# Two transformer layers on one core: a new out-projection, third norm, hand-over and routed block

## What is computed

```python
# layer 0
xn = layernorm(x)
x  = x + attn0(xn) + ffn0(xn)   # 32 query heads, 8 key heads of 64, window 64, rms norm, rotation; gated quantised ffn of 704
# layer 1
xn = layernorm(x)
Xn = layernorm(xn) * ln_w + ln_b
x  = x + (softmax(rope(Q) rope(K)^T / 4) V) W_out + xn \
       + routed(xn)             # attn1: 16 heads of 16, all 1024 keys
# routed: w = xn W_r + b_r; of each batch the 64 rows with the largest w;
#   rows with w above the 64th value become w * (gelu(x W1 + b1) W2 + b2), all others stay x
```

## Time and profile before

| what | value |
|---|---|
| median of 3 runs | 1092.83 us (1084.54, 1092.83, 1093.44) |
| the profiled execution | 1086.89 us, its span 1085.1 us |
| busy | PE 943.4, DVE 862.2, POOL 698.1, ACT 687.0 us |
| mean granted TensorE clock | 0.958 |

### The profile page before, as it was taken

The page is one execution under the profiler, slowest core; times in us unless marked ns, Lnnn a source line. Parts: engine busy times, 40 slices in busy tenths (PEclk is TensorE's granted clock), DMA queues, the critical chain, the costliest instruction groups (busy, mean ns, idle before and its releaser), DMA issues. The chain is left out here.

```text
span 1085.1 us, 26423 instructions
## 1 busy us (share of the span) xinstructions
PE 943.4 (87%) x8729; PEld 529.8 (49%) x8729; DVE 862.2 (79%) x1777; ACT 687.0 (63%) x1786; POOL 698.1 (64%) x1001
## 2 busy tenths in 40 slices
PE   3588997998988988989889887379999999999998
PEld 2355665665766656656667654243222222333233
DVE  6797888888887887887888883358999999888952
ACT  2555655655565655655656552016999999888974
POOL 4677888888888887887887882422655565332220
PEclk9698999999999999999999998579999999999999
DMA  5646544544444434444534432521121211311001
GB/s 193 126 106 123 108 90 86 97 83 91 95 82 90 96 81 91 97 79 88 102 80 87 93 82 52 166 65 21 22 42 21 40 22 22 50 31 36 7 2 39
DMA packets 241611, 81.00 MB, mean 75 GB/s; under 512 B 215812, under 2 KB 240068, under 8 KB 241220
## 3 DMA queue, kind: packets, MB, share of 16 engines
q1 hardware_dynamic: 238980, 74.85, 33.7%
q10 hardware_dynamic: 2496, 4.46, 1.2%
HBM read 18.49 MB, written 4.19 MB: 21 GB/s over the span
## 5 line engine op out<-in xcount | busy, mean ns | idle before, releaser
L1259 DVE TENSOR_REDUCE l_mxv<-l_mx 128x1 f32<-128x1024 f32 x256 | 294.9, 1217 | 28.1 <-PE l_mx L1462 28.1
L1170 ACT ACTIVATE l_prob<-l_sc 128x512 f32<-128x512 f32 x512 | 272.9, 604 | 30.1 <-PE l_sc L1470 29.1
L389 ACT ACTIVATE an<-an 128x256 f16<-128x256 f32 x128 | 53.3, 416 | 210.9 <-DVE an L563 210.5
L708 POOL TENSOR_TENSOR t<-t 128x320 f32<-128x320 f32 x128 | 110.3, 862 | 106.7 <-DVE t L610 106.5
L1462 PE MATMUL l_mx<-l_kt,l_qt 48*128 48x512 f16 x512 | 155.4, 386 | 13.6 <-DVE l_mxv L1259 13.6
L1470 PE MATMUL l_sc<-l_qt,l_kt 50*128 50x512 f16 x512 | 156.8, 384 | 0.4 <-ACT l_prob L1170 0.4
L699 POOL TENSOR_TENSOR rm<-ss,half_neg 128x5 f32<-128x5 f32 x128 | 155.9, 1218 | 0.0
L1441 PE MATMUL l_acc<-l_prob,qkv_all 128*17 128x256 f32 x2048 | 154.5, 386 | 0.0
L867 PE MATMUL ob<-wo_hi,ats 128*128 128x256 f16 x512 | 109.0, 280 | 32.8 <-DMA ats<-an 27.3
L1332 POOL TENSOR_SCALAR l_mxs<-l_mxv 128x8 f32<-128x8 f32 x32 | 7.5, 235 | 179.4 <-DVE l_mxv L1259 179.4
L812 PE MATMUL pv<-v,probs 128*64 128x65 f32 x2048 | 89.2, 230 | 30.0 <-ACT probs L438 23.0
(11 more groups left out here) (180 smaller groups left out, 2147.3 us busy)
## 6 DMA issues: line engine op xcount, KB each, us to landing
qkv_all<-w_qkv SPq DMA_DIRECT2D x3, 768.0 KB, 8.6
v<-v SPq DMA_DIRECT2D x64, 32.5 KB, 1.9
xn_all<-xs SPq DMA_DIRECT2D x16, 128.5 KB, 2.2
xa<-x SPq DMA_DIRECT2D x16, 128.0 KB, 2.4
tk<-nat SPq DMA_TRANSPOSE x128, 2.7
qkv_all<-w_o SPq DMA_DIRECT2D x8, 256.0 KB, 3.8
ats<-an SPq DMA_TRANSPOSE x128, 2.3
xc<-x SPq DMA_DIRECT2D x16, 128.0 KB, 2.5
```

Of the source, the lines that this page charges most:

```text
L389: return act.activation(dst, src, ACT.Copy, scale=scale)
L708: pool.tensor_tensor(t1[:, b, :, :], t1[:, b, :, :], t2[:, :, :], ALU.add).then_inc(s_["pool_u"], 1)
L1170: act.activation(prob[:, (y * NI + u) % NPR, h * 512:(h + 1) * 512], sc[:, k % NSC, :], ACT.Exp, scale=D1 ** -0.5).then_inc(s_["act_sc"], 1)
L1259: dve.tensor_reduce(mxv[:, x % 2, u:u + 1], mx[:, MX[k] % 2, :], AX.X, ALU.max).then_inc(s_["dve_mx"], 1)
```

## The change

1. Third norm: `norm_stats` on `xs` goes. Its variance is worked out from the second inverse root (1 + eps - eps x rs2^2: two DVE instructions on 128x1). `xl1` is one DVE instruction with `rs3` and `ln_w`; POOL keeps the addition of `ln_b`, and DVE has it for the last tile. POOL's rotation of tile 14 is moved by three slots, behind the last `rs3`.
2. Hand-over: the fp16 halves of items' pair 0 (`c = 0, 1`) are made by POOL inside layer 0 and turned by the last two DMAs of its SP queue; their memory is that of layer 0's projection weights (`early`). The small constants are loaded in layer 0 at slot 24. The router column is stored ahead of `xs`.
3. Routed block: thresholds, selection and positions go into slots 5 (`LEVEL_AT`, `PICK_AT`, `THR_AT`, `COUNT_AT`) behind the first maxima. Running sums replace the 28 counting matmuls by 1. The weighted one-hot matrix goes; the block is multiplied by the weight instead and split to fp16. Score banks are used beside `acc`, gelu's table is loaded at the start, `x1s` is loaded in four parts in slots 6 to 9.
4. Projections: POOL writes normalised items 0 to 23 as high and low fp16 halves (`ctx0`, `ctx1`) and splits `W_out`; SP turns them by DMA. Y is at `u == 3` of slots 25 to 32, Z at the eight places of `AHEAD_AT`. C and T go, with the copies behind them.

```diff
-SLOT_O = 25
-SLOT_H = 37
+SLOT_Y = 25
+AHEAD_AT = ((33, 3), (34, 3), (35, 3), (36, 3), (37, 2), (37, 5), (38, 1), (38, 4))
-SPREAD_AT = ((4, 6), (5, 0))
-GATHER_AT = ((5, 1), (5, 2), (5, 3), (5, 4))
-TURN_AT = (5, 6)
-HIDDEN_AT = ((6, 0), (6, 2))
+LEVEL_AT, PICK_AT = (5, 0), (5, 1)
+THR_AT, COUNT_AT = (5, 1), (5, 2)
+GATHER_AT = ((5, 3), (5, 4), (5, 5), (5, 6))
+TURN_AT = (5, 7)
+HIDDEN_AT = ((6, 0), (6, 1), (6, 2), (6, 3))
+SPREAD_AT = ((6, 4), (6, 6))
 RESULT_AT = ((6, 5), (6, 7))
+BLOCK_AT, PARTS_AT = (7, 0), ((7, 2), (7, 4))
...
+                    dve.scalar_tensor_tensor(mv3[:, par, :], rs2[:, par, :], -LN_EPS, rs2[:, par, :], ALU.mult, ALU.mult
+                                             ).then_inc(s_["dve_b3"], 1)
...
+                    dve.tensor_scalar(ve3[:, par, :], mv3[:, par, :], 1.0 + LN_EPS, None, ALU.add).then_inc(s_["dve_v3"], 1)
-                    norm_stats(st3, mv3, ve3, xs[:, par, 0:D], par, "dve_b3", "dve_g3", "dve_v3", n)
...
-                    pool.tensor_tensor(xl1[:, :], xl1[:, :], lnw[:, :], ALU.mult).then_inc(s_["pool_lw"], 1)
...
+                if s == way(NT - 1):
+                    pool.wait_ge(front["set_nq"], 2)
+                    pool.wait_ge(s_["pool_rope"], NT - 1)
+                    for c in range(2):
+                        split(pool, c, qkv1_all, nq, front)
...
+            sp.wait_ge(front["pool_split"], 2)
+            for a, dst in enumerate((qt, kt)):
+                sp.dma_start_transpose(dst[:, 0, :].rearrange("p (i t) -> p i t", i=NI),
+                                       nq[:, 0, a, :, :, :].rearrange("p i h e -> p (i h e)")).then_inc(wq_ld[a * 2], 16)
...
+                if (c, u) == COUNT_AT:
+                    pe.wait_ge(s_["mod_dve"], MOD["run8"])
+                    pe.matmul(counts, bef[:, :], sel, start=True, stop=False)
+                    pe.matmul(counts, ones[:, :], cum, start=False, stop=True).then_inc(s_["mod_pe"], 1)
...
+                pool.tensor_copy(parts[:, :, 0, d:d + D1], ctn[:, b, :, :]).then_inc(s_["pool_part"], 1)
+                pool.wait_ge(s_["pool_part"], t * 2 + 2)
+                pool.tensor_tensor(parts[:, :, 1, d:d + D1], ctn[:, b, :, :], parts[:, :, 0, d:d + D1], ALU.subtract
+                                   ).then_inc(s_["pool_ctx"], 1)
...
                         for j in range(KC):
-                            pe.matmul(mx[:, MX[k] % 2, 0:D], ctt[:, i % 2, j, :], wou[:, j, :], start=(j == 0), stop=False)
-                        pe.matmul(mx[:, MX[k] % 2, 0:D], spread[0:CAP, i, :], blk[0:CAP, :], start=False, stop=True
-                                  ).then_inc(s_["pe_mx"], 1)
+                            for n, (l, w) in enumerate(((0, wou_hi), (0, wou_lo), (1, wou_hi))):
+                                pe.matmul(mx[:, MX[k] % 2, 0:D], ctt0[:, i, l, j, :], w[:, j, :], start=(j == 0 and n == 0), stop=False)
+                        routed(mx[:, MX[k] % 2, 0:D], 0, i).then_inc(s_["pe_mx"], 1)
```

More of the change, by code:

```diff
@@ L90, in build @@
         qkv1_all = ctx.enter_context(nc.sbuf_tensor("qkv1_all", [P, ITEMS * NI * (2 * D1 + VW)], F32))
-        loads = layer0(nc, ctx, idf, idh, ranked, xn2_all, qkv1_all, x, w_qkv, w_o, q_w, k_w, w_gate, w_up, s_gate, s_up, w_down, s_down,
-               ln_w, ln_b, w_in, w_r, b_r, pos_table, masks, eye, out)
-        layer1(nc, loads, idf, idh, ranked, xn2_all, qkv1_all, w_out1, b_r, w1, b1, w2, b2, before, slots, out)
+        early = ctx.enter_context(nc.sbuf_tensor("early", [P, 2 * KC * G * CW], F16))
@@ new lines, in build, with turning @@
+        loads, spare = layer0(nc, ctx, idf, idh, ranked, xn2_all, qkv1_all, early, small, sources, front, x, w_qkv, w_o, q_w, k_w,
+                       w_gate, w_up, s_gate, s_up, w_down, s_down, ln_w, ln_b, w_in, w_r, b_r, pos_table, masks, eye, out)
+        layer1(nc, loads, spare, idf, idh, ranked, xn2_all, qkv1_all, early, small, front, w_out1, w1, w2, out)
+def turning(early):
+    nq = early[:, 0:4 * NI * P].rearrange("p (a j i h e) -> p a j i h e", a=2, j=2, i=NI, h=2)
+    qt = early[:, 4 * NI * P:4 * NI * P + 4 * S].rearrange("p (n s) -> p n s", n=4)
+    kt = early[:, 4 * NI * P + 4 * S:4 * NI * P + 8 * S].rearrange("p (n s) -> p n s", n=4)
+    return nq, qt, kt
@@ L952, in ahead @@
 def ahead(c, u):
-    return (c - SLOT_H) * NI + u
+    return AHEAD_AT.index((c, u)) if (c, u) in AHEAD_AT else None
 def fold_at(c, u):
@@ L985, in max_units, with layer1 @@
                 order.append(("X", c - LAG_X, u))
-            if u == 3 and 0 <= c - SLOT_O - 1 < NI:
-                order.append(("Y", c - SLOT_O - 1))
-            order += [(kind, i) for kind, i in (("Z", ahead(c, u) - 1), ("T", ahead(c, u))) if 0 <= i < NI]
+            if u == 3 and 0 <= c - SLOT_Y < NI:
+                order.append(("Y", c - SLOT_Y))
+            if ahead(c, u) is not None:
+                order.append(("Z", ahead(c, u)))
     return {unit: k for k, unit in enumerate(order)}
-def layer1(nc, loads, idf, idh, ranked, xn2_all, qkv1_all, w_out1, b_r, w1, b1, w2, b2, before, slots, out):
+def layer1(nc, loads, spare, idf, idh, ranked, xn2_all, qkv1_all, early, small, front, w_out1, w1, w2, out):
     SC = score_units()
@@ L1443, in piece, with routed @@
                 ins.then_inc(s_["pe_pv"], 1)
+            def routed(dst, b, i):
+                rows = slice(b * CAP, (b + 1) * CAP)
+                pe.matmul(dst, spread[rows, i, :], blk_hi[rows, :], start=False, stop=False)
+                return pe.matmul(dst, spread[rows, i, :], blk_lo[rows, :], start=False, stop=True)
             for c in range(SLOTS):
```

379 lines of the change are left out of this document (205 added, 174 removed).

## The result

The changed kernel takes **1047.9 us** (median of four: 1043.5, 1047.9, 1047.9, 1049.2) against 1093.1 for the kernel before, timed beside it; the ratio is 0.959 (95% interval 0.954 to 0.963). The prediction was 1048, range 1032 to 1064. Medians here are over all executions of a kernel; ratios and their intervals leave out the slow ones, more than 1.5% above its fastest.

The account below looks back on a forecast made before the run. No engine alone bounded layer 0, a chain of waits the hole behind it, PE the slots with projections; -5.0 (layer 0), -22.6 (head) and -13.7 (projections) make -41.3, from a mean of 1089.4 to 1048 us, range 1032 to 1064.

Parts of the forecast that it names:

- Layer 0's body: Third norm in layer 0's sixteen tiles: shorter DVE work saves 5.0 us in all, bounds 0 and 8.
- so not all arrives: I take 5.5: Third norm, layer 0: of 7.2 us saved on DVE over 16 tiles, 5.5 arrives, as PE is 91% busy.
- POOL's product with `ln_w` I count at nothing: Layer 0's tiles: taking this product, 0.72 us a tile, off POOL gains nothing, since POOL afterwards waits for DVE.
- layer 0 gains nothing: Rival on layer 0's body: PE is its bound, or `xl1` stretches by the shared interface; 1053 us, chance 0.16.
- the rival's price: `xl1` in layer 0: 0.94 us instead of 0.59 by the shared interface, 5.6 us over 16 tiles; that rival's chance 0.16.
- The end of layer 0: Last tile: `rs3` no longer waits for tile 14's rotation, PE transposes at 677.6 instead of 681.79; 4.2 us earlier.
- To the first maxima: Last rotation to first maxima: keys turned inside layer 0, constants' loads and 28 matmuls gone from the wait; -20.7 us.
- Slots 5 to 7: Start of layer 1: +1.1 us to slot 7 with the selection now inside, +1.2 in slot 7 from added DVE instructions.
- half clock through slot 5: Part of the slow-head rival: PE at half clock in slot 5, +6 us; with late transposes 1057 us, chance 0.15.
- Y and Z: Layer 1's projections as fp16 matmuls: Y slots 10.6 us, Z slots 10.3, slot 37 10.8; -13.7 in all.
- five fp16 matmuls, 0.55 + 0.24 = 0.8: Z in slots 33 to 36: each lengthens the 9.52 us slot by 0.8, to 10.3; +3.1 over the four.
- The floor of 9.95: Y slots: the least length, DVE's steady 9.52 us plus one add of 0.42; rival of slots there 1042 us, chance 0.16.

Follow-up runs that it names:

- mult_back: The changed kernel with the third norm's product with `ln_w`, and the last tile's addition of `ln_b`, back on POOL; 1054.8 us, ratio 0.970 to the kernel before.
- y_u6: The changed kernel with Y, and Z of slots 33 to 36, at the slot's seventh place instead of its fourth; 1051.6 us, ratio 0.965 to the kernel before.
- stats_back: The changed kernel with the third norm's statistics computed from the normed row again; 1061.5 us, ratio 0.973 to the kernel before.

## Why the prediction was right, and where not

**Layer 0's body** was mis-sized: -5.0 with bounds 0 and 8, where the marks give -9.0 and the ten middle tiles 0.59 a tile between the two kernels, 8.9 over fifteen. Two steps failed. The first and larger is "so not all arrives: I take 5.5". The statistics alone are worth 0.52 a tile, 7.8 over fifteen: all of the 0.45 a tile that the prediction had found arrives, and a little more. The second is "POOL's product with `ln_w` I count at nothing: it stands in a slot where POOL afterwards waits for DVE". POOL does wait there, 1.16 us in one tile of the changed kernel:

```profile
311.39 0.72 POOL L808 TENSOR_TENSOR xl<-xl,lnb 128x256 f32<-128x256 f32 x1
313.28 0.87 POOL L752 TENSOR_TENSOR t<-t 128x320 f32<-128x320 f32 x1 [1.16 <-DVE t L648]
```

But the wait is for DVE, and DVE in turn waits longer for ACT, as the groups above show, when the product is in POOL's queue. It is worth 0.17 a tile in the middle of the layer, 2.5 over fifteen; by the medians it is about 5.8 (1054.8 less 1047, less 2.0 at the end of layer 0), and where the other 3 lie is open. A later wait on the same engine didn't hide the instruction from the other engines. The rival "layer 0 gains nothing" is excluded.

The total came out right in spite of it, and that closeness is luck, since the misses cancel: from 1090.7, the middle one of the five medians of the kernel before in this study, 1.3 above the base taken, -41.3 as forecast, -4.0 more for the body and +2.7 for what slots 8 to 38 gave less make 1048.1; the mean of the changed kernel's eight executions is 1047.0. Each miss alone would have left the total within 5 us.

On the stretch of `xl1`: its median rose from 592 ns in the earlier trace rows to 902:

```profile
L706 DVE SCALAR_TENSOR_TENSOR xl<-xs,rs,lnw x16: 454/902/1074, 109.1 to 667.2; 128x256 f32<-128x256 f32 x16
```

The medians overstate it: the sixteen together take 11.7 us for 9.7, 0.13 a tile, where the prediction had 0.35 as the rival's price. With the product back on POOL (mult_back) `xl1` reads one SBUF tensor at the same place, and its median is 772, its sum 9.6. The Trainium skill (GPSIMD Engine Reference, section Specifications) says that GpSimd shares its SBUF interfaces with VectorE where the latter has two SBUF inputs; those 0.13 us agree with it in direction. The body gained its 9 us all the same; whether it would have gained more without this isn't shown.

**The end of layer 0** (-4.6 for -4.2) was right. Each of two edits is needed: with the product back on POOL, or the rotation of tile 14 in its old place, the last rotation ends 3.7 or 3.8 us later, so either alone gives little. No run undoes both. The number is in part luck: TensorE's transposes stand 5.5 us behind the residual instead of 9.2, which is 3.6 of the 4.2 forecast, and the splits weren't free, as the last rotation follows them without a gap at 673.6. The rest of the 4.6 has a reason that was not foreseen. Coming out of a short wait (0.52 us) TensorE runs at 2.4 GHz, and the four matmuls of L955 take 1.98; behind 3.65 us of waiting in mult_back the same four take 3.78, at 1.2 GHz, as the kernel before had them (3.59):

```profile
680.78 0.69 PE L946 MATMUL extra<-idf,xl 128*128 128x128 f32 x2 [3.65 <-POOL xl L807]
681.94 3.78 PE L954 MATMUL extra<-win,xt 128*128 128x512 f32 x4 [0.47 <-ACT xt L427]
```

**To the first maxima** (-20.2 for -20.7) was right, and its parts are now known: 9 us are the turning inside layer 0, about 8 that the constants don't land behind the weights (20 if the late clock of that variant belongs to it), 2 the place of the selection. They don't add up to the whole: undone one by one they may overlap, and the 28 matmuls' 6 us were not undone.

**Slots 5 to 7** (+0.9 and +0.8 for +1.1 and +1.2) were right, in a profile with the early clock. The rival "half clock through slot 5" was named with +6 and exists: it costs 12.4 us (42.0 less 29.6) and reaches through slot 6. Of the eleven profiles in which neither the turning nor the constants were put back, three have it; the eight timed executions of the changed kernel itself are all below 1052.

**Y and Z.** The Y slot is 10.64 for 10.6, but the reason given for it (the matmuls' own time) is only a part: a Z slot, with three fewer, takes 10.64 too, where 10.3 was forecast. The step that failed is "five fp16 matmuls, 0.55 + 0.24 = 0.8". At this place the slot pays for the buffer that the extra unit takes, not for its matmuls. Slot 38 came out at +2.2 for +1.4 too; slot 37 came out at 10.3 for 10.8. The floor of 9.95 was never near. POOL has 26.2 to 27.9 us in 40, 6.2 to 6.6 a slot, as forecast (6.7). The fp16 form itself was not undone; its gain is read from the slots.

## What to carry to other kernels

An instruction isn't free because its own engine waits later: follow the engines that wait for what stands behind it in the queue. When executions scatter by more than an edit is worth, look for the stretch in which they don't, here ten tiles in the middle of a layer, good to 1 us in 387. Where two buffers rotate, a short extra unit costs its place, not its length; place it where the consumer has the most lead. And what a DMA costs at a stage's start depends on what was issued in the same microseconds: five small loads and two transposes, put back one at a time behind the barrier between the layers, cost at least 8 and 9 us.

## What was not expected of the hardware

- The return of TensorE's clock after a wait varied from 10 to 39 us after the first maxima between profiles of kernels with nearly the same work there, with the engine busy in nearly all of it (2.00 of 2 us in the windows above). The late return costs 12.4 us, more than any single edit in the body; in y_u6, whose profile has it, two of the four executions of one program stand 12 us above the other two. The Trainium skill (TensorE: Matmul & The Clock Gate, section "What's actually happening") has it that activity releases the throttle. The clock did come back here each time, but the busy time that the profile shows doesn't say when.
- An instruction on 128x1 elements took 160 ns in the last tile, but 471 in the median over the sixteen (L686), while the instruction behind it took 402 instead of the 630 it has in stats_back, where nothing stands in front of it: it looks as if a stall is booked on whichever instruction stands first, but no run separates the two.
